# A fused attention and mixture-of-experts block on one core: the expert choice in fewer VectorE operations at another place of the step, ranks inside a batch from TensorE, and the left-over row scatters tied to the shared expert's groups

## The reference, cut to what matters

```python
x = x + tanh(g_xattn) * xattn(layernorm(x), ctx)     # 16 heads of 64, q and k layer-normed
h = layernorm(x)
probs = softmax(h @ Wg)                              # 8 experts
vals, idx = top_k(probs, 2)
weights = vals / (sum(vals) + 1e-9)
y = sum over the two chosen e: weights[e] * (silu(h @ W1[e] + b1[e]) @ W2[e] + b2[e])
shared = silu(h @ Ws1 + bs1) @ Ws2 + bs2
x = x + tanh(g_ffn) * (y + 0.1 * shared)
```

## Time and profile before

| | us |
|---|---|
| median of 3 runs (713.71 to 716.74) | 715.66 |
| the profiled execution's own time | 712.84 |
| its span (first to last instruction) | 710.8 |

### The profile page before, as it was taken

The page is one execution under the profiler, slowest core; times in us unless marked ns, Lnnn a source line. Parts: engine busy times, 40 slices in busy tenths (PEclk is TensorE's granted clock), DMA queues, the critical chain, the costliest instruction groups (busy, mean ns, idle before and its releaser), DMA issues.

```text
span 710.8 us, 21126 instructions
## 1 busy us (share of the span) xinstructions
PE 585.2 (82%) x7614; PEld 519.6 (73%) x7614; DVE 490.7 (69%) x1045; ACT 453.8 (64%) x982; POOL 362.4 (51%) x706
## 2 busy tenths in 40 slices
PE   3889999999789799889789877753889898989850
PEld 1678888888578677678677666643879898989850
DVE  5688898989889889889989874534324444444427
ACT  4588889998688688778778654430425454545425
POOL 3455555655446456667766653657002444545540
PEclk9799999999999999999999999977899999999985
DMA  6800101001001001001000000113201222222218
GB/s 240 256 2 3 32 18 32 18 2 47 3 17 32 17 11 54 8 17 56 9 18 10 10 16 17 39 37 136 61 0 39 69 69 69 73 67 77 70 63 326
DMA packets 22582, 38.01 MB, mean 53 GB/s; under 512 B 5232, under 2 KB 13040, under 8 KB 22352
## 3 DMA queue, kind: packets, MB, share of 16 engines
q1 hardware_dynamic: 17648, 27.27, 12.0%
q0 software_dynamic: 4544, 9.38, 3.7%
q10 hardware_dynamic: 288, 0.00, 0.0%
HBM read 23.17 MB, written 13.47 MB: 52 GB/s over the span
## 4 chain that ended last, share of the span: by engine, by line
PE 57%; DVE 22%; issue 8%; another core or an unknown queue 4%; ACT 4%; DMA 3%; POOL 1%; SPq 0%; ACTq 0%; DVEq 0%; POOLq 0%
PE ps L1333 8%; PE ps L1111 5%; PE ps L1137 5%; PE ps L1079 4%; PE ps L1120 4%; PE ps L1081 4%; PE ps L1080 4%; PE ps L1167 4%; PE ps L1319 3%; DVE sm L767 3%; PE ps L1321 3%; PE ps L1235 3%; DVE wide L745 3%; PE ps L1152 3%
## 5 line engine op out<-in xcount | busy, mean ns | idle before, releaser
L661 POOL DMA_INDIRECT results<-spo,xs_ix x78 | 75.4, 966 | 116.9 <-DVE spo L1053 102.0
L398 ACT ACTIVATE qk_T<-ps,lnw 128x512 f32<-128x512 f32 x128 | 96.7, 787 | 45.3 <-PE ps L1111 44.8
L517 ACT ACTIVATE qk_T<-ps,b_cols 128x256 f32<-128x256 f32 x156 | 61.9, 475 | 77.1 <-PE ps L1321 74.2
L1111 PE MATMUL ps<-ident,wide 128*128 128x128 f32 x512 | 80.3, 283 | 35.6 <-DVE x_res L721 34.2
L1111 PEld LDWEIGHTS ps<-ident,wide 128*128 128x128 f32 x512 | 60.3, 148 | 53.5 <-DVE x_res L721 42.2
L1079 PE MATMUL ps<-w_hi,xc_hi 128*128 128x512 f32 x192 | 89.9, 468 | 8.1 <-DVE wide L745 3.9
L745 DVE TENSOR_TENSOR wide<-ps,rstd 128x512 f32<-128x512 f32 x128 | 87.1, 681 | 4.4 <-POOL rstd L607 4.4
L738 DVE TENSOR_REDUCE ss<-wide 128x16 f32<-128x1024 f32 x64 | 77.6, 1212 | 11.1 <-ACT wide L374 10.8
L1081 PE MATMUL ps<-w_hi,xc_lo 128*128 128x512 f32 x192 | 78.9, 411 | 0.0
L374 ACT ACTIVATE wide<-ps 128x512 f32<-128x512 f32 x128 | 76.0, 595 | 3.6 <-PE ps L1081 3.5
L1080 PE MATMUL ps<-w_lo,xc_hi 128*128 128x512 f32 x192 | 78.1, 407 | 0.0
(11 more groups left out here) (171 smaller groups left out, 1387.3 us busy)
## 6 DMA issues: line engine op xcount, KB each, us to landing
v_sb<-routed SPq DMA_DIRECT2D x39, 130.0 KB
xc_in<-in_x SPq DMA_DIRECT2D x8, 256.0 KB, 3.0
xc_in<-in_ctx SPq DMA_DIRECT2D x8, 256.0 KB, 4.6
w_raw<-in_L_ffn_W SPq DMA_DIRECT2D x8, 256.0 KB, 2.6
wide<-results SPq DMA_DIRECT2D x4, 512.0 KB, 5.0
rows_all<-results SPq DMA_DIRECT2D x4, 512.0 KB, 8.3
out_x<-x_res SPq DMA_DIRECT2D x8, 256.0 KB, 4.2
x_res<-in_x SPq DMA_DIRECT2D x1, 1792.0 KB, 8.7
```

The source lines that it names most:

```text
L398: nc.scalar.activation(qk_T[:, n, 4 * j:4 * j + 4, :].rearrange("p a n -> p (a n)"), ps[6 + j][:, :], ACT.Identity, bias=lnw[:, 2 * n + 1: ...
L661: gp_.indirect_dma_start(out=results[:, :], out_offset=bass.IndirectOffsetOnAxis(ap=xs_ix[:, b4, a:a + 1], axis=0), in_=yb[:, b4, a, :], i ...
L1111: last = nc.tensor.transpose(ps[6 + j][:, a * P:(a + 1) * P], qk_n[:, n, c0:c0 + P], ident[:, :])
```

## The change

Four things are changed together. (1) VectorE's `route` moves from the middle of the step (between `row_inverses` and `residual`) to its end, behind `keep_logits`, with lag 11 in place of 12, so the batches 0 to 2 are routed in steps 11 to 34. (2) The choice is made on logits less the highest, without probabilities; the weights come from the exponentials in closed form; a batch takes 22 VectorE operations in place of 34, in phases 0 to 6, and ScalarE computes one more exponential of 8 columns (`second_exponentials`). (3) Ranks inside the batch come from TensorE: nine matmuls that accumulate in PSUM replace the two, and `fill_ranks` goes. (4) SCATTER_LAG is 17, so tiles 0 to 18 are scattered in the loop; tiles 19 to 31 follow behind it, and from the third of them on every second tile (four indirect DMAs) waits for h_done of one more shared group. One operation is added to the schedule of row tiles.

```diff
-        SCATTER_LAG = 20
+        SCATTER_LAG = 17
+        ROUTE_LAG = 11
...
-                nc.scalar.activation(gp, gp, ACT.Exp).then_inc(f_exp, 1)
+                nc.scalar.activation(ge, gp, ACT.Exp).then_inc(f_exp, 1)
+
+            def second_exponentials(b):
+                sc.wait_ge(f_top, b + 1)
+                nc.scalar.activation(e1, top, ACT.Exp).then_inc(f_e1, 1)
...
+                if b is not None and at == 2:
+                    second_exponentials(b)
...
             expert_exponentials(NB - 1)
+            second_exponentials(NB - 1)
...
-            for t in range(LAST_STEP - SCATTER_LAG + 1, TILES):
+            rest = range(LAST_STEP - SCATTER_LAG + 1, TILES)
+            for i, t in enumerate(rest):
+                g, odd = divmod(i, 2)
+                if odd == 0 and g >= 1:
+                    gp_.wait_ge(h_done, CH * min(g, GROUPS))
                 scatter(t)
...
             first_of = first_e[:, :].unsqueeze(1).to_broadcast([P, BT, E])
-            pad_rows = BT // 2
-
             def less_highest(b):
                 ve.wait_ge(lg_ready, BT * (b + 1))
                 lg = lg_all[:, BT * b:BT * b + BT, :]
                 after(nc.vector.tensor_reduce(gm, lg, AX.X, ALU.max))
                 nc.vector.tensor_tensor(gp, lg, by_expert(gm), ALU.subtract).then_inc(f_sub, 1)
-
-            def expert_probabilities(b):
+                ve.wait_ge(f_sub, b + 1)
+                after(nc.vector.scalar_tensor_tensor(tie, gp, 0.0, first_of, ALU.is_equal, ALU.mult))
+
+            def first_choice(b):
+                first = rows_all[:, BT * b:BT * b + BT, D + 1]
+                after(nc.vector.tensor_reduce(first, tie, AX.X, ALU.max))
+                after(nc.vector.tensor_tensor(oh[:, 0, :, :], tie, by_expert(first), ALU.is_equal))
+                after(nc.vector.scalar_tensor_tensor(rest, oh[:, 0, :, :], -3.0e38, gp, ALU.mult, ALU.add))
+
+            def highest_of_rest(b):
+                nc.vector.tensor_reduce(top, rest, AX.X, ALU.max).then_inc(f_top, 1)
+                ve.wait_ge(f_top, b + 1)
+                after(nc.vector.tensor_tensor(tie, rest, by_expert(top), ALU.is_equal))
+                after(nc.vector.tensor_tensor(tie, tie, first_of, ALU.mult))
+
+            def second_choice(b):
+                after(nc.vector.tensor_reduce(lead, tie, AX.X, ALU.max))
+                after(nc.vector.tensor_tensor(oh[:, 1, :, :], tie, by_expert(lead), ALU.is_equal))
+                nc.vector.tensor_tensor(picked[:, 0:BT, :], oh[:, 0, :, :], oh[:, 1, :, :], ALU.add).then_inc(f_cnt, 1)
+
+            def take_ranks(b):
+                ve.wait_ge(f_rank, b + 1)
+                nc.vector.tensor_tensor(rank, ps[5][:, E:E + BT * E].rearrange("p (j e) -> p j e", j=BT),
+                                        base[:, b, :].unsqueeze(1).to_broadcast([P, BT, E]), ALU.add).then_inc(f_taken, 1)
+                nc.vector.tensor_tensor(base[:, b + 1, :], ps[5][:, E + BT * E:2 * E + BT * E], base[:, b, :], ALU.add).then_inc(f_taken, 1)
+
+            def place(b):
+                ve.wait_ge(f_taken, 2 * b + 2)
+                after(nc.vector.tensor_tensor(hit, oh, rank.unsqueeze(1).to_broadcast([P, 2, BT, E]), ALU.mult))
+                with nc.allow_low_precision("slots are whole numbers"):
+                    nc.vector.tensor_reduce(slot[:, b, :, :], hit, AX.X, ALU.add).then_inc(f_slot, 1)
+
+            def denominators(b):
                 ve.wait_ge(f_exp, b + 1)
-                after(nc.vector.tensor_reduce(gs, gp, AX.X, ALU.add))
-                after(nc.vector.reciprocal(gs, gs))
-                after(nc.vector.tensor_tensor(gp, gp, by_expert(gs), ALU.mult))
-
-            def highest(c, probs):
-                after(nc.vector.tensor_reduce(top[:, c, :], probs, AX.X, ALU.max))
-
-            def ties(c, probs):
-                after(nc.vector.tensor_tensor(tie, probs, by_expert(top[:, c, :]), ALU.is_equal))
-
-            def chosen(c):
-                after(nc.vector.tensor_tensor(tie, tie, first_of, ALU.mult))
-                after(nc.vector.tensor_reduce(lead[:, c, :], tie, AX.X, ALU.max))
-                after(nc.vector.tensor_tensor(oh[:, c, :, :], tie, by_expert(lead[:, c, :]), ALU.is_equal))
-
-            def without_first():
-                after(nc.vector.scalar_tensor_tensor(rest, oh[:, 0, :, :], -2.0, gp, ALU.mult, ALU.add))
-
-            def count(b):
-                after(nc.vector.tensor_tensor(fill[0][:, pad_rows:, :], oh[:, 0, :, :], oh[:, 1, :, :], ALU.add))
-                with nc.allow_low_precision("counts up to 16 are exact"):
-                    nc.vector.tensor_reduce(cnt_b[:, b, :], fill[0][:, pad_rows:, :].rearrange("p j e -> p e j"), AX.X, ALU.add).then_inc(f_cnt, 1)
-
-            def fill_ranks(b):
-                after(nc.vector.tensor_copy(fill[1][:, pad_rows + 1:, :], fill[0][:, pad_rows:pad_rows + BT - 1, :]))
-                for n, sh in enumerate((1, 2, 4)):
-                    src, dst = fill[1 - n % 2], fill[n % 2]
-                    if n == 0:
-                        ve.wait_ge(f_cnt, b + 1)
-                    after(nc.vector.tensor_tensor(dst[:, pad_rows:, :], src[:, pad_rows:, :], src[:, pad_rows - sh:pad_rows + BT - sh, :], ALU.add))
-
-            def name_first(b):
-                after(nc.vector.tensor_scalar(rows_all[:, BT * b:BT * b + BT, D + 1], lead[:, 0, :], -1.0, float(E), ALU.mult, ALU.add))
+                after(nc.vector.tensor_reduce(gs, ge, AX.X, ALU.add))
+                after(nc.vector.tensor_scalar(den, gs, TOPK_EPS, 1.0, ALU.mult, ALU.add))
+                ve.wait_ge(f_e1, b + 1)
+                after(nc.vector.tensor_tensor(den, den, e1, ALU.add))
 
             def weigh(b):
                 tiles = slice(BT * b, BT * b + BT)
-                after(nc.vector.tensor_scalar(gs, top[:, 0, :], TOPK_EPS, None, ALU.add))
-                after(nc.vector.tensor_tensor(gs, gs, top[:, 1, :], ALU.add))
-                after(nc.vector.reciprocal(gs, gs))
-                for c in range(2):
-                    after(nc.vector.scalar_tensor_tensor(wtok[:, tiles, c], top[:, c, :], tg[:, 1:2], gs, ALU.mult, ALU.mult))
-
-            def take_ranks(b):
-                ve.wait_ge(f_rank, b + 1)
-                nc.vector.tensor_tensor(mine, ps[5][:, E:2 * E], base[:, b, :], ALU.add).then_inc(f_taken, 1)
-                nc.vector.tensor_tensor(base[:, b + 1, :], ps[5][:, 2 * E:3 * E], base[:, b, :], ALU.add).then_inc(f_taken, 1)
-
-            def place(b):
-                ve.wait_ge(f_taken, 2 * b + 2)
-                after(nc.vector.tensor_tensor(rank, fill[0][:, pad_rows:, :], mine.unsqueeze(1).to_broadcast([P, BT, E]), ALU.add))
-                after(nc.vector.tensor_tensor(hit, oh, rank.unsqueeze(1).to_broadcast([P, 2, BT, E]), ALU.mult))
-                after(nc.vector.tensor_reduce(slotf, hit, AX.X, ALU.add))
-                nc.vector.tensor_copy(slot[:, b, :, :], slotf).then_inc(f_slot, 1)
+                after(nc.vector.reciprocal(den, den))
+                after(nc.vector.tensor_scalar(wtok[:, tiles, 0], den, tg[:, 1:2], None, ALU.mult))
+                after(nc.vector.tensor_tensor(wtok[:, tiles, 1], wtok[:, tiles, 0], e1, ALU.mult))
 
...
                 if at == 1:
-                    expert_probabilities(b)
-                    highest(0, gp)
-                    ties(0, gp)
+                    first_choice(b)
                 if at == 2:
-                    chosen(0)
-                    without_first()
-                    highest(1, rest)
+                    highest_of_rest(b)
                 if at == 3:
-                    ties(1, rest)
-                    chosen(1)
-                if at == 4:
-                    count(b)
+                    second_choice(b)
+                if at == RANKS_AT:
+                    place(b)
                 if at == 5:
-                    fill_ranks(b)
-                    name_first(b)
+                    denominators(b)
                 if at == 6:
-                    place(b)
-                if at == 7:
                     weigh(b)
...
                 sum_squares(0, s + 1)
                 scale(1, 0, s)
                 row_sums(s - 1)
                 row_inverses(s - 1)
-                route(s, 12)
                 if s == TILES:
                     lo_part(0)
                 residual(s - 2)
...
                 less_maximum_of(0, s)
-                route_ranks(s, 12)
+                route_ranks(s, ROUTE_LAG)
                 keep_logits(s - 4)
+                route(s, ROUTE_LAG)
...
             less_highest(NB - 1)
             lo_part(2)
-            expert_probabilities(NB - 1)
-            highest(0, gp)
-            ties(0, gp)
-            chosen(0)
-            without_first()
-            highest(1, rest)
-            ties(1, rest)
-            chosen(1)
-            count(NB - 1)
-            fill_ranks(NB - 1)
-            name_first(NB - 1)
+            first_choice(NB - 1)
+            highest_of_rest(NB - 1)
```

(11 more changed lines are left out.)

40 lines of the change are left out of this document (18 added, 22 removed).

## The result

The changed kernel takes 672.66 us (median of 4 runs, 671.6 to 674.34), the kernel before 714.68 in the same set (4 runs, 708.88 to 716.74): ratio 0.943, interval 0.937 to 0.949. The forecast was 672.0. The profiled execution took 673.58, with a span of 671.8 us against 710.8.

What follows compares the result with a forecast made beforehand. TensorE was taken to bound the bare step, with routing costing 45.5 us in the loop. From 712.84 profiled, -28.4 in the loop and -15 behind it gave 669.4, with 2.8 for the median 672; eight in ten from 655 to 692.

Steps and rivals of the forecast that it cites:

- Out of the middle of the step: Loop: moving the router from between row_inverses and residual recovers all 45.5 us that routing costs, clock losses included.
- The clock: TensorE in the loop: short stretches at 1.2 GHz behind idle time vanish, leaving the clock full through the loop.
- At the step's end: Router's new place: 0.8 us for three operations plus 0.4 for the port, less 0.6 of cover: 0.6 us a step.
- The rival in which the port follows the router: At the step's end GpSimd's small operations block VectorE: 1.6 us a phase, loop gains only 13, total 688; chance 0.1.
- With scatters: Loop steps from 17 on: rstd of k comes late, 0.4 us more, 1.0 in all a step, for 12 phases.
- my 17.1: Routed loop steps' growth over the bare pace: 15.6 us for the router's new place and scatters, 1.5 for TensorE's ranks.
- TensorE's ranks: Seven more small matmuls a batch, 0.5 us each batch, 1.5 in the loop; the last batch's lie under a wait.
- Behind the loop: Shorter scatter rows cut TensorE's idle time by about 5.5 and 9.5 us, sum -15; bounds nothing and -22.9.
- the waits end with the rows of scatters: Behind the loop: ScalarE and VectorE come back about 2.3 and 2.7 us behind the ends of unbroken scatter rows.
- at most one wait would exceed 5 us: Sign of being right behind the loop: at most one wait without a releaser longer than 5 us.
- my -43.4: Whole kernel: -28.4 us in the loop and -15 behind it, from 712.84 to 669.4 by the profile.

Runs made afterwards that it cites:

- e1: The kernel before with its 34 router operations unchanged but moved to the end of VectorE's step (lag 11): 690.82 us, ratio 0.969.
- e2: The changed kernel with its fewer router operations back at the old mid-step place (lag 12), scatters as before: 701.15 us, ratio 0.981.
- e4: The changed kernel with the loop's scatters issued behind second_rstd instead of first in GpSimd's step: 668.49 us, ratio 0.934.
- e3: The changed kernel with before's scatter schedule (lag 20, no waits between groups): 687.01 us, ratio 0.960; again on another chip 632.57 us.
- the third chip: The chip of the last four runs: the changed kernel, unaltered, took 633.0 us there, ratio 0.9425; the kernel before 672.0 us (13 runs).

## Why the prediction was right, and where it was not

**Out of the middle of the step: right.** e1 shows it alone; the block with L618 on GpSimd is in 16 phases of e2, and in none at the new place. The clock came back with it, as forecast: granted 1.00 from 202.76 to 403.93 us, where the 20 steps of before had 0.97. The Trainium skill (page "SBUF — State Buffer", section "SBUF: two separate sides") has VectorE and GpSimd exclude each other for a whole instruction where VectorE's has two inputs from SBUF and GpSimd's reads SBUF. By that rule, the 1.95 us of L809 under the 1.90 of L618 agree. At the new place L824 and L825 ran beside L575 at their bare 0.23 us, which the rule would not have let me expect; there the measurement decides.

**"At the step's end": mis-sized.** I booked 0.8 for three operations and 0.4 for the port, less 0.6 of cover. The port's part measured 0. The 4 steps without scatters (I had counted 6, but the scatters begin in the fifth) grew by 46.25 - 4 x 11.16 = 1.6 us, 0.4 each for my 0.6. The rival in which the port follows the router is refuted.

**"With scatters": the step that failed.** I took 0.4 us more, for a `rstd` that would come late in GpSimd. The 16 steps with scatters grew by 201.2 - 178.6 = 22.6 us, 1.4 each with the ranks among them. What they have in place of a late `rstd` are gaps in TensorE's issue under the scatters (9.2 us listed, 19 us in all on the rows of scores), a mechanism that the prediction did not name. That the scatters are its cause is shown three ways: the rows are whole in the steps without scatters, whole but for 1.2 us of gaps where e4 moves the scatters, and in e3 the long steps begin with the first scatter. The rows of before could not show it, for in the routed step shown the first scatter stood under TensorE's waiting and none beside the scores. On a chip without the gaps the loop came out at 233.1, that is 9.9 above the bare 223.2; my 17.1 stood between 9.9 and 24.2.

**"TensorE's ranks": right in size.** All nine matmuls of a batch run from 306.28 to 306.66 in the loop, 0.4 us, where I took 0.5 for the seven that are new. In the last batch, under a dense row, they took 3.1 us (436.25 to 439.35), under a wait as said.

**"Behind the loop": right in the sum, by two errors that cancel.** The idle time ahead of `shared_out` went from 25.8 us (four waits) to 4.6, 21.2 gained where I took 15. But 6.7 us came new, in gaps of TensorE's issue at L1207, L1178 and L1194 (2.6, 2.2 and 1.9). Table row 3 has the net: 14.8 less. That the waits end with the rows of scatters held again (row's end at 439.92, L469 and L935 back at 442.1). It was not as strict as I read it: in before VectorE came back at 468.45, 2.6 us ahead of the end of the first row (471.0), and only ScalarE behind it. That at most one wait would exceed 5 us was wrong: five do (8.35, 7.26, 7.14, 6.88, 5.29), though only two of them are that long behind their inputs. The Trainium skill (page "Runtime: NRT & Kernel Launch", section "Instruction fetch mechanics") has each engine's instructions come ahead of it through a DMA queue of its own, hidden behind the rate of issue. By that rule, the third chip agrees (1.16 us for 64 matmuls); on the first, gaps of 9.2 us and waits to 8.4 would contradict it if they were late instructions. Their kind, "issue" and no releaser, suggests that, but the DMA records of the same trace speak against it. They hold the packets of the instruction queues with their times: while ScalarE and VectorE stood until 442.1 none came (one ended at 430.0, the next began at 453.4), nor during the first long pair of e3 (none from 428.3 to 459.5), and the row of scores at 301.55 has its two gaps with no such packet near it. What it is that the engines wait for stays open.

**The total.** -21.3, -15.8 and -1.9 (an earlier loop, for which I booked nothing) give -39.0 by the spans against my -43.4: by the profile I had 669.4, and it was 673.58. That 672.0 met 672.66 is partly luck: I added 2.8 us for the median, which lay above the profiled execution before and 0.9 below it after. The loop gained 7.1 us too little, and 2.7 of that came back at the smaller items.

**What stays open.** Which mechanism holds the engines up, as said. Whether pacing every tile's scatters removes the rest of the waits on a chip of the first kind: it was tried only where there were none. Nor is it known which property of a chip makes them, or whether it is the chip at all and not the sitting: a chip measured twice would tell. No version here is shown to beat the changed kernel on both kinds.

## What to carry to other kernels

An operation that meets another engine's long one pays once for the place, not by the count of its neighbours: move it first, shorten it second. When the wait that bounds a loop is removed, look at what the new bound shares with others; costs that slack had hidden, here gaps in TensorE's issue in 16 steps, appear only then and could not be read from the trace of before. When a wait has no releaser, see first when its inputs ended; what is left may be a quarter of the figure in brackets. And put the kernel before, and the changed one, beside every experiment on the same chip: the same gain of 5.7% came once as 21 us in the loop and 16 behind it, and once as 37 and 3.

## What the runs showed of the hardware

Sets of runs on different chips of one type differ by 6% in this kernel: before took 714.68 and 714.26 us in two sets of runs and 671.48 and 672.0 in two others, the changed kernel 672.66 and 633.0. The difference is in three things: ScalarE's and VectorE's waits without a releaser behind the loop; the rows of scores under the loop's scatters, seen once the router has left the middle of the step (changed kernel, 1.9 to 2.5 us against 1.16 to 1.22); and the routed tiles, which take 142.9 to 145.7 us on the first kind and 133.8 to 135.1 on the other. In all three GpSimd issues indirect DMAs. Among the routed tiles it is VectorE that stops without a releaser on the first kind, and TensorE waits for it, 7.8 us against 1.6. Their waits there, of the changed kernel as first measured (494 to 637 us) and then on the third chip (466 to 600):

```profile
PE ps L1303 <- DVE w_lo L1003: 7.8, 4, 2.1
...
DVE w_lo L1003 <- issue: 11.7, 8, 2.2
```

```profile
PE ps L1303 <- DVE w_lo L1003: 1.6, 1, 1.6
...
DVE w_hi L1018 <- issue: 0.7, 2, 0.3
```

In the loop of before, where TensorE has slack, the two differ by no more than 1.3 us (268.7 and 270.0).
